# Expert tiles: the order of TensorE's up and down products within a turn

## The reference

```python
route = sigmoid(x @ Wr + br);  max_prob = max(route);  max_ind = argmax(route)
for e in range(8):
    y = gelu(x @ W1[e]) @ W2[e]          # W1: 128 -> 512, W2: 512 -> 128
    out = out + (max_ind == e) * y
x = layernorm(x + out * max_prob)
```

## Time and profile before

| | |
|---|---|
| median of 3 runs | 1606.0 us (1604.95 to 1606.63) |
| the profiled execution's own time | 1602.92 us |
| its span, first to last instruction | 1601.1 us |
| mean granted TensorE clock | 0.945 of full speed |
| PE / PEld busy | 1432.7 / 876.0 us |
| DVE / ACT / POOL busy | 1270.1 / 1087.6 / 1252.1 us |
| transfers | 236.92 MB, mean 148 GB/s |

### The profile page before, as it was taken

How to read it: one execution, slowest core, us unless ns; L and a number is a source line. 1 busy time by engine, 2 the same in 40 slices (tenths; PEclk the granted TensorE clock), 3 DMA queues, 4 the chain that set the end, 5 groups by cost and what they waited for, 6 DMA issues and landing times. The chain is left out here.

```text
span 1601.1 us, 22049 instructions
## 1 busy us (share of the span) xinstructions
PE 1432.7 (89%) x6146; PEld 876.0 (55%) x6146; DVE 1270.1 (79%) x2207; ACT 1087.6 (68%) x2118; POOL 1252.1 (78%) x861
## 2 busy tenths in 40 slices
PE   4888998999999989998997799999999999639994
PEld 1333343334434433433343378888788887539993
DVE  1899999999999999999999557777877778835442
ACT  4778878887888788878886467666666665314552
POOL 1799999999999999999999644467777776735665
PEclk8899999999999999999999979999999999869997
DMA  5455454545555554564455174133326200047771
GB/s 169 148 172 174 166 184 178 182 171 181 180 169 183 181 174 157 184 191 177 158 171 181 30 249 143 53 118 138 113 75 255 100 15 8 20 123 196 205 210 36
DMA packets 126058, 236.92 MB, mean 148 GB/s; under 512 B 13490, under 2 KB 76917, under 8 KB 125952
## 3 DMA queue, kind: packets, MB, share of 16 engines
q1 hardware_dynamic: 121408, 227.21, 43.4%
q0 software_dynamic: 4544, 8.47, 1.6%
HBM read 180.89 MB, written 55.66 MB: 148 GB/s over the span
## 5 line engine op out<-in xcount | busy, mean ns | idle before, releaser
L401 POOL TENSOR_TENSOR hc<-state,c_rows 128x1024 f32<-128x1024 f32 x256 | 598.7, 2359 | 49.4 <-DVE state L598 40.2
L598 DVE TENSOR_TENSOR_SCAN state<-ps_da,inp 128x512 f32<-128x512 f32 x512 | 593.4, 1206 | 29.6 <-ACT ps_da L494 29.6
L717 PE MATMUL ps_y<-hc,ident 128*128 128x512 f32 x1024 | 493.3, 621 | 55.4 <-POOL hc L401 55.3
L494 ACT ACTIVATE ps_da<-dt,a_neg 128x512 f32<-128x512 f32 x512 | 345.4, 688 | 82.8 <-DVE state L598 81.0
L717 PEld LDWEIGHTS ps_y<-hc,ident 128*128 128x128 f32 x1024 | 194.9, 197 | 297.6 <-issue 213.1
L587 DVE TENSOR_TENSOR inp<-dtx,ps_b 128x1024 f32<-128x1024 f32 x192 | 230.8, 1202 | 37.9 <-POOL dtx L372 22.3
L1082 POOL TENSOR_TENSOR rs<-ms,m_half 128x4 f32<-128x4 f32 x48 | 67.9, 1415 | 121.8 <-DVE ms L1303 121.6
L1220 ACT ACTIVATE ex<-sc,nmx,ctx_r 77x128 f32<-77x128 f32 x192 | 92.4, 482 | 101.1 <-DVE nmx L1316 101.1
L384 POOL TENSOR_TENSOR inp<-dtx,b_rows 128x1024 f32<-128x1024 f32 x64 | 150.9, 2358 | 0.1
L640 PE MATMUL ps_misc<-x1T,w_conv 128*128 128x512 f32 (+3 forms) x256 | 119.2, 611 | 20.6 <-ACT x1T L427 20.6
L500 ACT COPY ps_b<-b_rows 128x512 f32<-128x512 f32 x192 | 111.1, 579 | 37.9 <-DVE inp L587 35.7
(11 more groups left out here) (234 smaller groups left out, 2690.6 us busy)
## 6 DMA issues: line engine op xcount, KB each, us to landing
b_rows<-bc_rows SPq DMA_DIRECT2D x128, 512.0 KB, 4.7
c_rows<-bc_rows SPq DMA_DIRECT2D x128, 512.0 KB, 3.9
sorted_x<-pad_rows SPq DMA_DIRECT2D x8, 4160.0 KB, 16.6
w<-in_L_ffn_W SPq DMA_DIRECT2D x78, 256.0 KB
vw<-vw_rows SPq DMA_DIRECT2D x16, 462.0 KB
vw_rows<-vw_out SPq DMA_DIRECT2D x16, 384.0 KB
xrow<-sorted_x SPq DMA_DIRECT2D x39, 130.0 KB, 2.3
x_tok<-in_x SPq DMA_DIRECT2D x16, 256.0 KB, 4.0
```

The costliest lines, as they stand in the source:

```text
L401: pool.tensor_tensor(hc[:, n % RING], state[:, n % RING], over_c(c_rows[:, slot, n % 2]), ALU.mult).then_inc(hc_ready, 1)
L494: act.activation(ps_da[u % DA_RING][:], dt[:, par, c], ACT.Exp, scale=a_neg[:, c, n:n + 1]).then_inc(da_ready, 1)
L598: dve.tensor_tensor_scan(state[:, n % RING, c], ps_da[u % DA_RING][:], inp[:, n % RING, c], 0.0, ALU.mult, ALU.add).then_inc(state_ready, 1)
L717: ins = pe.matmul(ps_y[:, c], ident[:], hc[:, n % RING, c], start=False, stop=n == NS - 1)
```

## The change

In PE's turn the down products of tile j-2 move ahead of the up products of tile j-1. Nothing else is changed: the same instructions, buffers, semaphores and waits, in another order on one engine.

```diff
         def tile(j, buf, turn, half):
 
             if within(j, 0):
                 transposed(j, buf, turn)
+            if within(j, 2):
+                down(j - 2, earlier(buf, turn, 2)[0])
             if within(j, 1):
                 up(j - 1, *earlier(buf, turn, 1))
-            if within(j, 2):
-                down(j - 2, earlier(buf, turn, 2)[0])
         over_tiles(pe, tile, 2)
```

## The result

| | before | after |
|---|---|---|
| median of 4 runs (lowest to highest) | 1606.32 us (1604.95 to 1607.51) | 1635.21 us (1633.74 to 1635.61) |
| the profiled execution's own time; span | 1602.92; 1601.1 us | 1634.95; 1633.1 us |
| mean granted clock | 0.945 | 0.947 |

The changed kernel is slower: the ratio is 1.0178, with a 95% interval of 1.0161 to 1.0196, which is 28.9 us (25.9 to 31.5). The forecast was 1637.0 us, 31.0 us more, in a range of 1629 to 1647.

What follows compares the result with a forecast made beforehand. PE was taken to bound the expert stage, full in turns of 3.73 us. 37 gaps of 0.74 us (27.4) plus 3.5 us for U(38)'s lost places made 31.0 us on a 1606.0 us median: 1637.0 us, range 1629 to 1647.

Steps and rivals of the forecast that it cites:

- PE sets the pace and has no gap to close: Expert stage before: PE's products fill the whole 3.73 us turn, so no order shortens it and reordering only opens gaps.
- D's stream begins 0.96 us after U's, a gap of 0.74 us: PE's turn: D waits 0.96 us after U's end for gelu1, release and weight load; T fills 0.22, 0.74 idle.
- What I said PE's record would show: Expert stage, PE or PEld: idle ahead of D each turn, about 0.7 to 0.9 us, 38 or 39 times.
- the rival of a mostly hidden gap: Gap ahead of D: release and weight load cost nothing, gap 0.58 us, 24.8 us in all, 1631 us; chance 10%.
- A turn of 4.47 us, 37 times: Expert stage, D(0) to D(37): each turn 0.96 + 1.78 + 1.73 = 4.47 us; the gaps total 27.4 us.
- D(0) at the same instant: Expert stage's start: D(0) already waited for tile 0's GELUs, so its stream still starts at about 1435.6 us.
- U(38) falls back by 31.0 us, and the end with it: Expert stage's end: U(38) comes 30.96 us later, and POOL's last chain moves with it by 31.0 us.
- The median: Whole kernel: the 31.0 us shift set beside the median of 1606.0 us gives 1637.0 us.
- The clock rival: Expert stage: gaps make PE's clock fall, 1767 us if in all 37 turns, 1702 in half; large form's chance 5%.
- The smaller form: Expert stage's start: PE idles 1.6 us until D(0), clock falls for one or two turns, 3.5 to 7 us.
- The POOL rival: Expert stage: POOL's queue sets the end and absorbs PE's gaps, so time stays at 1606 us; chance 3%.
- none of these adds to the gap: PE's turn: D's other wait, DVE's copy, SP's loads and POOL, which has room, add nothing to the 0.74 us.

Runs made afterwards that it cites:

- e1: Changed kernel with D summed chunk by chunk over both row halves, waiting for gelu1 only ahead of chunk 2; 1606.41 us, 1.001 to the kernel before.
- e4: Changed kernel with D(j-3) in place of D(j-2) ahead of U, so D comes one tile later; 1604.56 us, 0.9993 to the kernel before.
- e7: Kernel before with ACT's normalisations of tile j-5 ahead of tile j's GELUs and POOL storing tile j-5 in place of j-6; 1603.20 us, 0.9986.
- e8: Kernel before with a spare GELU of the second half, read by nobody, ahead of gelu1; 1606.49 us, 1.0007.
- e11: Kernel before with D one tile later and ahead of U, ACT's normalisations first and POOL storing tile j-5 in place of j-6; 1602.78 us, 0.9985.
- e5: Changed kernel with ACT's normalisations of tile j-5 ahead of the GELUs of tile j; 1642.01 us, 1.0221 to the kernel before.
- e9: Changed kernel with ACT's normalisations first and POOL storing tile j-5 in place of j-6; 1632.57 us, 1.0163 to the kernel before.
- e10: Changed kernel with POOL's stores of tiles j-7 and j-6 gathered, four in a row in each even turn; 1648.58 us, 1.0262 to the kernel before.
- e6: Changed kernel with a spare GELU of the second half, read by nobody, ahead of gelu1; 1654.48 us, 1.0315 to the kernel before.

## Why the prediction was right, point by point

- *PE sets the pace and has no gap to close.* Right: turns of 3.73 us before, and every variant without a gap (e1, e4, e7, e8, e11) has them again, none has shorter ones.
- *D's stream begins 0.96 us after U's, a gap of 0.74 us.* Right in size and in its parts: 0.20 to gelu1, 0.60 of gelu1, 0.05 of release and 0.11 of weight load. The row that carried the last two terms came from another stage and another shape. What I said PE's record would show, 0.7 to 0.9 us of idle time, it shows on PEld (0.70) but not on PE (0.47), since PE's records overlap. The same rows rule out the rival of a mostly hidden gap, 0.58 us.
- *A turn of 4.47 us, 37 times.* Right to 0.01 us in most turns. Where PE's loop begins anew, every sixth turn, T to T was 4.54 us (1520.38 to 1524.92): 0.3 to 0.4 us in all that the sum does not have.
- *D(0) at the same instant.* D(0)'s first weight load is 6.05 us after T(0), and was 5.91. But the reading behind it was wrong, and this term came out right by luck: in the kernel before D(0) did not wait for the GELUs, it followed U(1) without a gap, 1433.95 + 1.73 = 1435.68:

```profile
1433.95 1.89 PE L1953 MATMUL ps_h<-xcol,w 128*128 128x256 f32 x8
1435.68 0.50 PE L1962 MATMUL ps_yy<-w,act_h 128*128 128x128 f32 x3
```

  Its weight load at 1435.48 stands 0.20 us ahead of its first product, as D(37)'s, which waits for nothing, stands 0.21 us ahead (1573.32 and 1573.53). That the GELUs of tile 0 ended at 1435.42, at almost the same time, is a coincidence.
- *U(38) falls back by 31.0 us, and the end with it.* The last gelu1 moved by 31.96, of which 0.57 is T(0)'s later start and 0.14 the start of D(0); 31.25 are left for 30.96. The tail behind it is 27.4 us in both. e5 and e9 showed that it hangs where the sum put it, on the normalisation of tile 33 behind gelu1: with that moved, the tail is 3.5 and 2.5 us shorter. POOL's list counts there too: in e10, with ACT's order unchanged, the tail is 26.4 us.
- *The median.* 1635.2 for 1637.0. By the stage lengths the change costs 31.4 us, by the medians 28.9 (25.9 to 31.5). The forecast's 31.0 lies in that interval; what the 1.8 us between forecast and median are made of, runs that differ by 3 us can't say.
- *The clock rival.* Did not happen: 1.00 from 1437 to 1600 us with a gap in every turn, so what the prediction cited from the Trainium skill ("TensorE: Matmul & The Clock Gate", section "A second HAM failure mode: psum-queue depth-cycling"), that small idle times can be enough, did not come about with gaps of 0.74 us in turns of 4.47. Nor did it with gaps of 1.23 us (0.74 + 0.49) in turns of 4.96: e6's clock is 1.00 from 1440 to 1600 us. The smaller form, a fall right after the start, didn't come either (D(0) and U(1) took 1.89 and 1.73 us), but it was hardly put to the test: PE's idle record ahead of D(0) is 0.72 us, not the 1.6 us of the prediction. And the prediction's argument against the rival was weaker than it looked. That the clock fell "only" where PE was down to 2.07 us of 4 is not so: elsewhere in the slot stage of the kernel before PE was busy 3.05 us of 4.00 up to 1084.81 us, with one idle time of 0.95 us, and the clock was 0.50 right behind that. So that it held here was not settled by the earlier trace rows. In e10, behind one of the late GELUs, PE's record shows 1.82 us of idle time, and the granted clock fell to 0.50, which is 1.2 GHz, for most of the D and U that followed (windows of e10):

```profile
1514.00:1516.00 2.00, 0.32 (x2) 0.32 (x3) 1.11 (x5) 1.46 (x4) 0.00 (x0) 1.00 0.75 248
1516.00:1518.00 2.00, 2.00 (x16) 2.00 (x15) 0.80 (x5) 0.39 (x2) 0.82 (x1) 0.72 0.32 71
1518.00:1520.00 2.00, 2.00 (x7) 1.64 (x7) 0.00 (x0) 0.00 (x0) 1.50 (x3) 0.50 0.56 154
```

  That turn's D and U took 5.3 us (1515.68 to 1520.96) in place of 3.6. It happened behind one such gap of seven in e10, and behind none of the seven in e5, whose clock is 1.00 from 1444 to 1576 us.
- *The POOL rival.* Did not happen: POOL's idle time ahead of its stores grew from 1.41 + 0.38 us for two tiles to 2.14 + 1.16, by the 1.5 us that were forecast. POOL had room, as the earlier trace rows said. But "none of these adds to the gap" was luck of spacing: in e10 the same stores in another rhythm make the stage 10.8 us longer, and I had weighed POOL only as a queue, not as something that can hold up its neighbours.

## What to carry to other kernels

When two groups of work on a full engine change places, count what is left between each producer and its consumer, and hold the round trip through the other engine against it: here 0.85 us of waiting and release, plus a weight load that is no longer hidden, against 0.22 us of transposes. A round trip that does not fit is paid once per turn, however idle the other engine is. Where an order must stay, let the consumer wait for the half that is ready (e1): that bought back all but 3.3 of the stage's 31.4 us.

## What I had not expected of the hardware

Four indirect stores of 128 rows in a row on POOL, 1.27 to 1.35 us apart, went with a late ACT (mostly 1.4 to 1.8 us), a late DVE (0.8 us in the turn shown) and a late SP (1.7 us there), mostly in every fourth turn (e5, e10). With a wait of POOL of 1.0 us or more between two and two no GELU was late, neither in the other groups of these two runs nor in e7 and e9. PE's own instructions started on time. Whether more rows, more stores or the loads beside them matter was not tried.
